# Cross-attention on one core: the weighted sums moved between the third score tile and the last maximum tile of a quad, the ones-product to the quad's end

## What is computed

```python
q = (x @ Wq + bq).reshape(B, N, NUM_HEADS, HEAD_DIM)
k = (y @ Wk + bk).reshape(B, M, NUM_HEADS, HEAD_DIM)
v = (y @ Wv + bv).reshape(B, M, NUM_HEADS, HEAD_DIM)
scores = jnp.einsum('bnhd,bmhd->bhnm', q, k) * scale
attn = jax.nn.softmax(scores, axis=-1)
out = jnp.einsum('bhnm,bmhd->bnhd', attn, v).reshape(B, N, IMAGE_DIM)
h = jax.nn.relu(out @ W1 + b1)
return h @ W2 + b2
```

## Time and profile before

| | |
|---|---|
| median of 3 runs | 1363.45 us (1362.64 to 1365.55) |
| the profiled execution | 1362.23 us, of which its span 1360.4 us |
| TensorE busy | 1297.9 us (95%) |
| VectorE busy | 1118.7 us (82%) |
| ScalarE busy | 976.4 us (72%) |
| GpSimd busy | 708.3 us (52%) |
| longest groups in attention | maxima R 590.2 us, GpSimd's sums 556.4 us, exponentials E 554.4 us |
| longest waits before maxima R | 64.0 us in all, nearly all for maximum tiles |

### The profile page before, as it was taken

How to read it: one execution, slowest core, us unless ns; L and a number is a source line. 1 busy time by engine, 2 the same in 40 slices (tenths; PEclk the granted TensorE clock), 3 DMA queues, 4 the chain that set the end, 5 groups by cost and what they waited for, 6 DMA issues and landing times. The chain is left out here.

```text
span 1360.4 us, 39341 instructions
## 1 busy us (share of the span) xinstructions
PE 1297.9 (95%) x16386; PEld 665.6 (49%) x16386; DVE 1118.7 (82%) x1819; ACT 976.4 (72%) x2002; POOL 708.3 (52%) x320
## 2 busy tenths in 40 slices
PE   7999999999899999999999999999999999999998
PEld 4444444444345444544544454454444445566454
DVE  5768888888898988898888988889887745678895
ACT  4454555544899999999999999999999931354332
POOL 0321221222688878978887888888789001111121
PEclk9999999999999999999999999999999999999999
DMA  7667777876452212122211212221211030492000
GB/s 262 188 167 203 214 228 209 226 215 171 136 170 63 64 59 70 39 70 67 53 57 57 69 40 70 69 69 40 67 59 32 4 148 1 108 212 32 1 9 24
DMA packets 127798, 137.49 MB, mean 101 GB/s; under 512 B 44995, under 2 KB 108995, under 8 KB 125699
## 3 DMA queue, kind: packets, MB, share of 16 engines
q1 hardware_dynamic: 127622, 134.98, 35.2%
HBM read 75.70 MB, written 44.17 MB: 88 GB/s over the span
## 5 line engine op out<-in xcount | busy, mean ns | idle before, releaser
L1380 DVE TENSOR_REDUCE early<-attend_banks 128x1 f32<-128x512 f32 x952 | 590.2, 682 | 64.0 <-PE attend_banks L1080 62.6
L1529 POOL TENSOR_TENSOR early<-early,attend_prob 128x1152 f32<-128x1152 f32 x210 | 556.4, 2650 | 65.6 <-ACT attend_prob L1337 46.1
L1337 ACT ACTIVATE attend_prob<-attend_banks 128x512 f32<-128x512 f32 x1024 | 554.4, 601 | 16.5 <-PE attend_banks L1120 9.0
L1120 PE MATMUL attend_banks<-early,k_first 97*32 97x512 f16 x2560 | 265.5, 380 | 2.9 <-ACT attend_prob L1337 1.6
L1080 PE MATMUL attend_banks<-k_first,early 96*32 96x512 f16 x2272 | 215.8, 380 | 9.0 <-DVE early L1380 7.7
L1293 ACT ACTIVATE attend_banks<-attend_banks,early 128x512 f32<-128x512 f32 x238 | 160.0, 672 | 18.3 <-DVE early L1380 18.3
L1120 PE MATMUL attend_banks<-early,attend_k_rest 97*32 97x512 f16 x1536 | 162.0, 380 | 1.1 <-ACT attend_prob L1337 0.9
L1080 PE MATMUL attend_banks<-attend_k_rest,early 96*32 96x512 f16 x1536 | 143.4, 380 | 8.9 <-DVE early L1380 8.9
L1133 PE MATMUL attend_banks<-attend_prob,attend_vh_odd 128*32 128x512 f32 x1024 | 135.6, 592 | 0.0
L1133 PE MATMUL attend_banks<-attend_prob,wkv_area 128*32 128x512 f32 x1024 | 135.6, 592 | 0.0
L1080 PEld LDWEIGHTS attend_banks<-k_first,early 96*32 96x32 f16 x2272 | 74.8, 95 | 113.9 <-DVE early L1380 91.8
(11 more groups left out here) (230 smaller groups left out, 1997.0 us busy)
## 6 DMA issues: line engine op xcount, KB each, us to landing
v_scratch<-project_v SPq DMA_DIRECT2D x16, 1024.0 KB, 8.9
early<-in_ctx_dram SPq DMA_DIRECT2D x16, 768.0 KB, 6.2
k_first<-k_scratch SPq DMA_DIRECT2D x36, 256.0 KB, 3.4
k_scratch<-project_k_hi SPq DMA_DIRECT2D x64, 128.0 KB, 3.0
k_scratch<-project_k_lo SPq DMA_DIRECT2D x64, 128.0 KB, 3.1
attend_vh_odd<-v_scratch SPq DMA_DIRECT2D x8, 1024.0 KB, 5.1
wkv_area<-v_scratch SPq DMA_DIRECT2D x7, 1024.0 KB, 5.0
attend_k_rest<-k_scratch SPq DMA_DIRECT2D x24, 256.0 KB, 3.4
```

Source lines behind the costliest of these rows:

```text
L1120: last = nc.tensor.matmul(s_ps[c * HD:(c + 1) * HD, s_bank(h, n), :], key_rows[:, c * HD:(c + 1) * HD], q_stack[0:KROWS + 1, h, :], start= ...
L1337: nc.scalar.activation(prob[:, q % PSLOTS, t, :], s_ps[:, s_bank(h, BT * q + t)], ACT.Exp).then_inc(p_ready, 1)
L1380: nc.vector.tensor_reduce(tile_low[:, s, j, part:part + 1], pre_ps[:, bank], AX.X, ALU.max, negate=True).then_inc(pre_read, 1)
L1529: nc.gpsimd.tensor_tensor(sums, sums, prob[:, q % PSLOTS, 0:POOL_TILES, 0:ADDED], ALU.add).then_inc(pool_summed, 1)
```

## The change

Two entries of the table change place, and PV becomes an entry of it:

```diff
-PE_ORDER = (0, (0,), 1, (3,), "den", 2, (1,), (2,), 3)
+PE_ORDER = (0, (0,), (3,), 1, (1,), 2, "pv", (2,), 3, "den")
...
                     if n - PRE_BANKS == turn_of["output"]:
                         wait(pe, o_scaled, h)
+                        if h == 0:
+                            pe.wait_ge(pre_summed, EARLY_SUMS + tiles_summed(0, n - 2 * PRE_BANKS))
...
+                            elif step == "pv":
+                                if q >= 1:
+                                    weighted(i, s, q - 1)
+                                elif not first:
+                                    weighted(*before, QUADS - 1)
                             elif isinstance(step, int):
                                 scores(i, s, q, step)
                             elif ahead(q, last):
                                 pre(i, s, q, *step)
-                        if q >= 1:
-                            weighted(i, s, q - 1)
-                        elif not first:
-                            weighted(*before, QUADS - 1)
```

## The result

| | before | after |
|---|---|---|
| median | 1363.72 us of 7 runs | 1368.42 us of 7 runs (1367.12 to 1369.37) |
| after to before | | 1.0032 (1.002 to 1.0044), +4.4 us (2.7 to 6.0) |
| the profiled execution | 1362.23 us, span 1360.4 us | 1368.42 us, span 1366.5 us |

A forecast was written before the change was run, and what follows sets the result against it. TensorE, back to back at 2.77 us per quad, was taken as the bound, a VectorE-ScalarE loop 0.04 under it. Costs +4.2 and last head -1.6 gave +2.6 us, median 1366.0, range 1362.8 to 1371.0.

The forecast's parts named there:

- Steady quads: Quads 0 to 1 and 6 to 14: loop through the later S1 takes 2.78 to 2.80 us; cost 0.14 us per head.
- The stalls of quads 2 and 3: VectorE stalls: the gap before P2 only moves to the next P0; between -0.02 and 0 us per head.
- Quad 5: Output product takes the bank behind X, so the next P0 comes later; cost 0.04 us per head (0 to 0.06).
- Quads 14 and 15: Later P2 of quad 13 delays R2, head maximum and R0 of quad 14; cost 0.11 us per head (0.05 to 0.15).
- E0: ScalarE's exponential of S0, not a run; at the head's end forecast 0.61 us after the copy of the row.
- The prediction's cover for PV: Steady quads: E3 of the quad before ends at 0.45 us, PV stands at 1.09; cover 0.6 us.
- The last head: Head 15, with the end of head 14: PV to PV falls from 2.26 to 2.18 us; -1.6 us (-0.8 to -2.5).
- D: Rival: TensorE stays the bound in steady quads, loop at 2.77 us or less; +0.6 us, 1364.0; chance 0.18.
- small C: Rival: steady quads' new loop somewhat longer than forecast, 2.80 or 2.81 us a quad; +4 to +6 us; chance 0.07.
- A: The forecast itself: the loop from X to P0 is the ring; +2.6 us, 1366.0; chance 0.60.
- B: Rival: the later P2 wins TensorE's waits for VectorE, 15.4 us less costs; -14.9 us, 1348.6; chance 0.07.
- full C: Rival: E1 follows S1 by 0.55 us, so steady quads' loop is 2.88 us; +14.5 us, 1378; chance 0.08.

The follow-up runs named there:

- the swap alone: In the kernel before, P3 put ahead of S1, with P1, PV and the ones-product left where they were; 1367.66 us, 1.003 against before.
- putting S1 back: In the changed kernel, S1 put ahead of P3 again, all else as changed; 1368.17 us, 1.003 against before.
- the share moved: VectorE's share of quad 3 placed behind R3 instead of before R0; 1351.07 us in the changed kernel, 1349.07 us in the kernel before.
- The better version: Kernel before with share and reciprocal behind R3, old order in heads 0 to 14, changed order in head 15 alone; 1346.15 us, 0.9873.
- the addition cut short: In the changed kernel, GpSimd's addition of quad 2 cut from 384 to 8 columns, share left in place; 1349.81 us, 0.9902 against before.
- after again: The changed kernel measured a second time, without any edit; 1368.5 us, 1.003 against before.
- the spread one: Kernel before with share and reciprocal behind R3, the share and all that hangs on it one quad later, in quad 4; 1348.07 us, 0.9886.
- the changed order with both moves: The changed kernel with the reciprocal of quad 2 and the share of quad 3 placed behind R3; 1352.6 us, 0.9916 against before.
- the old order with both moves: The kernel before with the reciprocal of quad 2 and the share of quad 3 placed behind R3; 1346.93 us, 0.9882.

## Why the prediction was right or wrong

**Steady quads: the mechanism right, the term too large.** The loop P0, P3, S1, E1, E2, X, P0 binds: the swap alone creates it, and putting S1 back removes it. It measured 2.778 or 2.779 us in quads 7 to 13, which is the low end of the 2.78 to 2.80 given, against the 2.771 that TensorE really took. The taken +0.015 a quad, 0.14 per head, was +0.009 on average over the nine quads, 0.08 per head (1.1 us in place of 2.0).

**The stalls of quads 2 and 3: half right, and the step that failed.** The statement that the gap before P2 only moves to the next P0 held: quad 2 changed by -0.03, and TensorE's waits for VectorE went over into waits for X. The Trainium skill, Perfetto Trace Analysis, section "Optimization Strategy", says to find the gaps of the most-contended engine and make what they wait for start sooner or finish faster. Moving P2 made nothing start sooner, and won nothing; moving the share did, for both P2 and X, and won 1.15 us per head (47.70 to 46.55). So the rule holds when what moves is the thing waited for, and the forecast was right in not expecting its gain from a move of the waiting tile.
What failed is the step "I cost both at nothing, between -0.02 and 0 per head" for quad 3. It held the share's 1.40 us for VectorE's own work, which no order on TensorE can change. It was a wait for the end of GpSimd's addition of quad 2, and the changed order delays that: the share takes 1.498 in place of 1.406, and quad 3 is 0.095 longer with the share where it was and not longer at all with the share moved. The prediction had noted that GpSimd's sums wait for E2, and drew nothing from it. Quads 1 to 4 together cost -0.004 - 0.031 + 0.095 + 0.030 = +0.09 per head, 1.3 us. Of these, quad 4's +0.030 stays with the share moved (2.842 and 2.808), and no run says what it is. That 16 elements took 1.40 us was to be seen in the earlier trace rows, beside a reciprocal of 128 elements at 0.96.

**Quad 5: right.** Predicted 0.04 per head, measured 0.037, and 0.038 with the swap alone.

**Quads 14 and 15: the size near, the mechanism wrong.** Predicted +0.11, measured +0.138 (0.051 + 0.087). The step was that the later P2 of quad 13 delays R2, the head maximum, and so R0 of quad 14 to 0.59 behind its P0. It does not. VectorE in after, R2 of quad 13, the head maximum and quad 14's maxima, with P0 of quad 14 on TensorE:

```profile
673.20 0.22 DVE L1390 TENSOR_REDUCE early<-early 128x4 f16<-128x64 f32 x1
673.34 2.61 DVE L1383 TENSOR_REDUCE early<-attend_banks 128x1 f32<-128x512 f32 x4
```

```profile
672.86 0.61 PE L1080 MATMUL attend_banks<-k_first,early 96*32 96x512 f16 x8
```

R0 starts 0.48 behind P0 (673.34 - 672.86), as it does in before (median 0.480 in both): the head maximum holds VectorE for 0.14 us and not 0.22. What quad 14 pays is the loop through S1 once more. X stands 1.851 behind P0 in place of 1.804, the row product and the next P0 come 0.05 later with it, and the swap alone, which leaves P2 where it was, gives the same +0.052. The larger cost stands in quad 15, which the swap alone leaves as it was (3.182), and which putting S1 back leaves long (3.314). There ScalarE, with the copy of the row behind E3, answers to the earlier trace rows:

```profile
675.28 0.21 ACT L1296 ACTIVATION_READ_ACCUMULATOR attend_banks<-attend_banks,early 128x1 f32 x1
675.47 0.60 ACT L1340 ACTIVATE attend_prob<-attend_banks 128x512 f32<-128x512 f32 x1
676.09 0.59 ACT L1290 ACTIVATE early<-attend_banks 1x512 f16<-1x512 f32 x1
676.71 0.60 ACT L1340 ACTIVATE attend_prob<-attend_banks 128x512 f32<-128x512 f32 x1
```

S3 stands behind PV now, at 675.02, so E3 can start at 675.47 and not sooner (0.45 behind it). The copy follows E3's start by 0.62 and the row product at 675.59 by 0.50, where it was 0.42 behind the product before. The copy waits for E3's end and not for the product, and E0, X of quad 15 and the P0 behind that wait behind the copy. Over heads 1 to 13 the copy comes 0.135 later (3.236 behind P0 of quad 14 in place of 3.101) and P0 of quad 15 only 0.051 later; the 0.084 between them are nearly all of quad 15's +0.087. This is read from the rows and from both swaps; no run moved S3 alone. The prediction's cover for PV, that E3 ends 0.6 ahead of it, was right, but behind E3 it had not looked for the copy.

**The last head: the sign right, the term too large.** In its full quads from the middle on PV to PV went to 2.18 as worked out, to be seen in after:

```profile
1092.79 1.03 PE L1135 MATMUL attend_banks<-attend_prob,attend_vh_odd 128*32 128x512 f32 x8
...
1094.97 1.03 PE L1135 MATMUL attend_banks<-attend_prob,attend_vh_odd 128*32 128x512 f32 x8
```

But not in all. After quads 8, 10 and 12 ScalarE does one more instruction, on the output of the earlier heads (line 1359), and one quad in two is longer there in either kernel. In after:

```profile
1080.37 0.71 ACT L1359 ACTIVATE attend_oT_halves<-attend_oT,late 128x512 f16<-128x512 f32 x1
1080.98 4.23 ACT L1340 ACTIVATE attend_prob<-attend_banks 128x512 f32<-128x512 f32 x8
1085.11 0.71 ACT L1359 ACTIVATE attend_oT_halves<-attend_oT,late 128x512 f16<-128x512 f32 x1
```

PV to PV alternates there between 2.18 and 2.56 us, before between 2.26 and 2.56. From one such instruction to the next, two quads take 4.74 us (1085.11 - 1080.37) in place of 4.82: 0.08 for two quads and not for each. This is the step that was too large: the prediction took the last full quad, which has no such extra, for all fifteen. Quad 1 stayed at 2.98 us from S0 to S0 (before 2.97); quad 2 went from 2.26 to 1.73, but quad 3 from 2.39 to 2.90, together no gain. What sets these is not shown.

Head 15 gained 0.73 us in place of 1.2, with 0.37 more in the last two quads of head 14 (2.31 to 2.20, 2.77 to 2.51), against some 0.4: 1.1 in place of 1.6. The better version gained as much and no more, 1.15. Its head 14 keeps the old order, so that the 0.37 falls into the first quad of head 15, which takes 1.89 us there, 2.26 before and 2.36 in after.

**The sum.** Terms as measured: 14 x (0.08 + 0.09 + 0.037 + 0.138) - 0.73 - 0.37 = 4.8 - 1.1 = +3.7 us, in place of 4.2 - 1.6 = +2.6. This agrees with the measured +4.4 (2.7 to 6.0). That the forecast came as near as it did is in part luck: the steady quads were taken 0.9 us too dear, which hid most of the 1.3 us that quads 1 to 4 cost. The ends of the stated range are also wider than their own working: D with 2.5 us in the last head gives 1363.15 and not 1362.8, small C with quad 14 at its upper end 1370.0 and not 1371.0. The measured 1368.42 lies inside either way. A stays the case that came true. B, a gain in VectorE's stalls, fell: quad 2 won 0.03 and quad 3 lost 0.095; full C would have shown 2.85 or more; D fell with the steady quads at 2.779 and the first swap. The remaining 2.5 us of the profiled +6.2 are a piece of the clock in head 0, below.

## What to carry to other kernels

Before a stalled instruction is moved away from its stall, find the second chain that comes to the same place: here P2's wait for VectorE and P0's wait for X both came out of one late R0, and moving P2 changed only the name of the wait. Ask of the operation at the head of such a stall whether its duration fits its size; one of 16 elements that takes 1.4 us is itself waiting, and one place later on its own engine it cost 0.17 us and gave back 17 us in the changed order and 14 in the old one, more than any order of TensorE tried here. A move of real work, as the reciprocal's 0.95 us, only shifts the bill to the next quad.

## What was not expected of the hardware

**VectorE's product of two SBUF operands ends with GpSimd's addition.** It ends 0.031 to 0.040 us after the end of the running addition in every head, and is 0.16 or 0.17 us long when there is none. Maxima R, which read a score bank, ran beside the same additions at 0.68 us each (median 681 ns).

**The clock at the start of the stage.** In after's profile TensorE's granted clock is 0.50, its 1.2 GHz level, for 6.83 us near the start of head 0. Windows of the same place in after, in the same order with the addition cut short, and in before; columns as in the earlier trace rows:

```profile
344.27:351.10 6.83, 6.66 (x60) 2.14 (x56) 4.39 (x8) 4.60 (x11) 1.89 (x1) 0.50 1.04 261
```

```profile
344.27:351.10 6.83, 6.08 (x100) 2.51 (x95) 5.99 (x10) 6.60 (x15) 2.04 (x1) 1.00 1.03 252
```

```profile
344.27:351.10 6.83, 6.17 (x99) 2.17 (x92) 6.39 (x11) 6.83 (x17) 2.65 (x1) 1.00 1.03 256
```

60 matmuls were issued there in place of 99 or 100. What TensorE did ahead of it, in after:

```profile
343.04 0.40 PE L1122 MATMUL attend_banks<-early,k_first 97*32 97x512 f16 x4 [1.29 <-PEq L296]
```

It had stood idle for 1.29 us. But so it had in before, where the clock stayed:

```profile
343.45 0.40 PE L1120 MATMUL attend_banks<-early,k_first 97*32 97x512 f16 x4 [1.30 <-PEq L296]
```

The same 1.3 us stand ahead of the first S0 in all twelve profiles, so this idle time alone does not decide it. Head 0 took 49.29 us; with the addition cut short and the clock full it took 45.46, and 1.15 of the difference is the share, so the piece cost some 2.7 us. The profiles show it in both orders (after, after again, the share moved in either kernel, the spread one, the changed order with both moves) and its absence in both orders (before, S1 first, P3 alone, the cut addition, the old order with both moves); the better version had 3.41 us of it. So it does not hang on the order alone, and it makes most of what the profiled +6.2 us has over the sum of +3.7.

It does not make the +4.4 us of the medians. Beside the second measurement of after, 5 of its 8 executions had a mean granted clock below 0.996, and 8 of the 17 of before on the same chip. Among those at 0.996 the medians are 1367.39 us (3 executions) and 1362.89 us (9), still 4.5 us apart. What makes the clock fall at this place in one execution and not in another is open.
